# A decoder block in FP32 on one core: projections written as four column tiles, cross-attention score products of two heads per load of the queries, and a new order of the work

## The reference, cut to what matters

```
x = x + SelfAttention(layernorm(x))              # 16 heads of 16, rotary positions
x = x + CrossAttention(layernorm(x), ctx)        # 16 heads of 16, 77 context tokens
x = x + FFN(layernorm(x))                        # 6 nodes, each an attention of 8 heads of 32:
    q,k,v = linear functions of earlier nodes' outputs
    node  = act_w * (softmax(q k^T / sqrt(32)) v) @ Wo + q ;  at the end a layernorm with gain and shift
```

## Time and profile before

| | |
|---|---|
| median of 3 runs | 5278.08 us (5269.1 to 5292.41) |
| the profiled execution: its time | 5268.01 us |
| its span, first to last instruction | 5266.2 us |
| PE busy / PEld busy | 4823.1 us (92%) / 3530.9 us (67%) |
| DVE / ACT / POOL busy | 3453.1 us (66%) / 2479.3 us (47%) / 707.9 us (13%) |
| mean granted TensorE clock | 0.962 of full speed |
| PE matmul records / all instructions | 59612 / 149908 |

### The profile page before, as it was taken

One profiled execution on the slowest core, in us unless ns is written; L12 is line 12 of the kernel. 1 busy time (PEld: TensorE's weight loads), 2 busy tenths in 40 slices (PEclk: granted clock), 3 DMA queues, 4 the chain that ended last, 5 costly groups with the idle time before them and its releaser, 6 DMA issues.

```text
span 5266.2 us, 149908 instructions
## 1 busy us (share of the span) xinstructions
PE 4823.1 (92%) x59612; PEld 3530.9 (67%) x59612; DVE 3453.1 (66%) x6058; ACT 2479.3 (47%) x4737; POOL 707.9 (13%) x1734
## 2 busy tenths in 40 slices
PE   7998999989899898998989989899998989989898
PEld 6676766757667676666767667676675767757676
DVE  3666676666766667676676766667666676666765
ACT  1454444545455454454544445454454544545444
POOL 0102011020211102111020110202102021120201
PEclk8999999999999999998999999999999999999999
DMA  3000000000000000000000000000000000000000
GB/s 120 5 2 11 2 11 3 2 11 2 11 3 2 11 2 11 2 6 7 2 11 2 6 7 2 11 2 11 2 2 11 2 11 3 2 11 2 8 2 6
DMA packets 42888, 44.64 MB, mean 8 GB/s; under 512 B 11552, under 2 KB 41888, under 8 KB 42144
## 3 DMA queue, kind: packets, MB, share of 16 engines
q1 hardware_dynamic: 34192, 26.55, 1.7%
q10 hardware_dynamic: 7952, 7.81, 0.4%
HBM read 25.96 MB, written 8.39 MB: 7 GB/s over the span
## 4 chain that ended last, share of the span: by engine, by line
issue 55%; PE 28%; DVE 7%; POOL 6%; ACT 1%; POOLq 1%; DVEq 0%; ACTq 0%
PE banks L945 27%; DVE row_max L909 3%; POOL neg_max L719 2%; POOL neg_max L722 2%; POOL x_tok L704 1%; POOL inv_std L698 1%; PE banks L1064 1%; DVE pair_sums L930 1%; ACT probs L818 1%; DVE rope_s L874 1%; DVE k_parts L887 0%; POOL var_eps L695 0%; PE banks L994 0%; DVE n_tok L930 0%; DVE x_tok L942 0%
## 5 line engine op out<-in xcount | busy, mean ns | idle before, releaser
L909 DVE TENSOR_REDUCE row_max<-banks 128x4 f32<-128x1024 f32 (+1 forms) x1280 | 1313.3, 1068 | 350.5 <-PE banks L945 348.0
L818 ACT ACTIVATE probs<-banks 128x1024 f32<-128x1024 f32 (+1 forms) x1280 | 1137.8, 935 | 487.6 <-PE banks L945 469.9
L945 PE MATMUL banks<-k_parts,q_parts 32*128 32x256 f32 (+1 forms) x15360 | 652.1, 306 | 166.8 <-DVE row_max L909 130.9
L945 PEld LDWEIGHTS banks<-k_parts,q_parts 32*128 32x128 f32 x15360 | 541.9, 201 | 333.7 <-DVE row_max L909 162.4
L930 DVE TENSOR_TENSOR pair_sums<-probs 128x512 f32<-128x512 f32 x512 | 368.1, 719 | 524.3 <-ACT probs L818 403.3
L945 PE MATMUL banks<-q_parts,k_parts 32*128 32x256 f32 (+1 forms) x13824 | 605.4, 304 | 75.1 <-DVE row_max L909 32.0
L945 PEld LDWEIGHTS banks<-q_parts,k_parts 32*128 32x128 f32 (+1 forms) x13824 | 470.6, 188 | 291.6 <-issue 163.4
L719 POOL TENSOR_TENSOR neg_max<-row_max,zeros 128x8 fp32r<-128x8 f32 x640 | 166.4, 260 | 3680.1 <-DVE row_max L909 3680.1
L945 PE MATMUL banks<-node_t,w_n 128*128 128x256 f32 x2560 | 633.2, 390 | 5.5 <-ACT node_t L835 5.5
L930 DVE TENSOR_TENSOR n_tok<-probs 128x512 f32<-128x512 f32 x512 | 364.2, 711 | 286.7 <-PE banks L945 167.9
L945 PEld LDWEIGHTS banks<-node_t,w_n 128*128 128x128 f32 x2560 | 461.4, 190 | 125.2 <-issue 46.1
(11 more groups left out here) (130 smaller groups left out, 6491.7 us busy)
## 6 DMA issues: line engine op xcount, KB each, us to landing
x_next<-in_x SPq DMA_DIRECT2D x32, 256.0 KB, 2.7
out_y<-x_tok SPq DMA_DIRECT2D x32, 256.0 KB, 2.1
w_head<-in_wf SPq DMA_DIRECT2D x11, 256.0 KB, 10.9
c_t<-in_ctx_t SPq DMA_DIRECT2D x32, 77.0 KB, 2.9
w_edge_t<-in_we_t ACTq DMA_DIRECT2D x9, 256.0 KB, 10.9
w_head<-in_wf ACTq DMA_DIRECT2D x7, 256.0 KB, 9.3
w_edge_t<-in_we_t SPq DMA_DIRECT2D x6, 256.0 KB, 9.1
w_n<-in_we ACTq DMA_DIRECT2D x3, 256.0 KB, 11.5
```

What stands on the lines that cost most here:

```text
L818: done(act.activation(probs[s][0:rows, g % 2, 2 * p:2 * p + 2, 0:kt, :] .rearrange("p c k t -> p c (k t)"), psum[0:rows, b0:b0 + 2, 0:kt * T],
L909: done(dve.reduce_max(row_max[s][:, g, 2 * p:2 * p + 2, :].rearrange("p c q -> p (c q)"), psum[:, b0:b0 + 2, :].rearrange("p c (q t) -> p ...
L945: return nc.tensor.matmul(bank_ap, lhs, rhs, start=start, stop=stop, **kw)
```

## The change

There are four edits and a new list.

1. `matmul_by_columns` takes the place of one whole-array product by four with 32 columns of the stationary operand each, written to four quarters of the partitions. `Q`, `QB`, `K`, `V`, `QR`, `KR`, `OA` and `OB` use it. `TR` and `MT` keep the whole array. (For the values of the context, with 77 rows, there are three tiles.)
2. In stage 1, `S` and `SB` stream the keys of both halves of a strip (2 x 78 columns) for one load of the queries. The groups 1 and 3 of `S`, `SB`, `MX` and `NM` are gone there; `ST` and `SX` keep four groups.
3. `MX` in stage 1 reduces both heads in one instruction (2 banks x 4 maxima of 77), with the same two instructions per group.
4. `NM` in stage 1 splits the maxima of both heads at once.
5. `ORDER` is new: 922 pieces in place of 942, other banks, other neighbours.

```diff
+def score_groups(j):
+
+    return range(0, groups(j), 2 if j == CROSS else 1)
...
-KI0.1 LNP0.1 V1.0@5 LNN0.1 KS1.0 TR0.1@3 KH0.1 KL0.1 TRE0.1 KH1.0 KL1.0 Q0.1@6 QB0.1 QH0.1.0 QH0.1.1 QL0.1.1
-QL0.1.0 VE1.0 S1.0.0@0 SB1.0.0 MX1.0.0.0 MX1.0.0.1 S1.0.1@4 SB1.0.1 MX1.0.1.0 MX1.0.1.1 S1.0.2@0 SB1.0.2
-MX1.0.2.1 S1.0.3@4 SB1.0.3 MX1.0.3.0 MX1.0.2.0 NM1.0.2 MX1.0.3.1 S0.1.0@0 SB0.1.0 MX0.1.0.1 MX0.1.0.0 NM1.0.3
-S0.1.1@4 SB0.1.1 MX0.1.1.0 NM1.0.1 MX0.1.1.1 S0.1.2@0 SB0.1.2 MX0.1.2.0 NM1.0.0 MX0.1.2.1 S0.1.3@4 SB0.1.3
-MX0.1.3.1 MX0.1.3.0 MT1.0.0@0 MT1.0.1@2 MR1.0.0 MR1.0.1 NM0.1.1 NM0.1.3 ST1.0.0@4 SX1.0.0 ST1.0.1@0 SX1.0.1
...
+KI0.1 LNP0.1 LNN0.1 KS1.0 V1.0@3 TR0.1@4 KH0.1 KL0.1 TRE0.1 KH1.0 KL1.0 Q0.1@7 QB0.1 VE1.0 QH0.1.0 QH0.1.1
+S1.0.0@0 SB1.0.0 QL0.1.0 QL0.1.1 S1.0.1@4 SB1.0.1 MX1.0.0.0 MX1.0.1.1 MX1.0.0.1 MX1.0.1.0 XB0.1 NM1.0.1 S1.0.2@0
+SB1.0.2 MX1.0.2.0 MX1.0.2.1 NM1.0.2 NM1.0.0 S1.0.3@4 SB1.0.3 MX1.0.3.1 S0.1.0@0 SB0.1.0 MX0.1.0.1 MX0.1.0.0
+MX1.0.3.0 NM1.0.3 S0.1.2@0 SB0.1.2 MX0.1.2.0 MX0.1.2.1 MT1.0.0@5 MR1.0.0 ST1.0.0@4 MT1.0.1@1 SX1.0.0 MR1.0.1
+ST1.0.1@0 SX1.0.1 EX1.0.0.0 PA1.0.0.0 EX1.0.0.1 PA1.0.0.1 PV1.0.0@7 PS1.0.0 NM0.1.0 MT0.1.0@6 EX1.0.1.0
...
 
+        def pair_max(s, g):
+
+            return row_max[s][:, g:g + 2, :, :].rearrange("p a c q -> p (a c q)").rearrange("p (c m) -> p c m", c=4)
...
-                negated = row_max[s][:, g, :, :]
                 parts = neg_max[s][:, u, :, :].rearrange("p q (c r) -> p c q r", c=4)
+                high, low = parts[:, :, :, 2 * i], parts[:, :, :, 2 * i + 1]
+                negated, zero = row_max[s][:, g, :, :], zeros[:, :, 0:QT]
+                if j == CROSS:
+                    both = parts[:, :, :, 0:4].rearrange("p c q (e i) -> p c q e i", i=2)
+                    high, low = both[..., 0], both[..., 1]
+                    negated = pair_max(s, g).rearrange("p c (q e) -> p c q e", q=QT)
+                    zero = zeros[:, :, :].rearrange("p c (q e) -> p c q e", q=QT)
                 pool.wait_ge(sem["max_taken"], reached(at, "max_taken", ("MX", s, j, g, 0), ("MX", s, j, g, 1)))
-                done(pool.tensor_tensor(parts[:, :, :, 2 * i], negated, zeros[:, :, :], ALU.add),
-                     "max_split", (a, "high"))
+                done(pool.tensor_tensor(high, negated, zero, ALU.add), "max_split", (a, "high"))
                 pool.wait_ge(sem["max_split"], reached(at, "max_split", (a, "high")))
-                done(pool.tensor_tensor(parts[:, :, :, 2 * i + 1], negated, parts[:, :, :, 2 * i].bitcast(F32),
-                                        ALU.subtract), "max_split", (a, "low"))
+                done(pool.tensor_tensor(low, negated, high.bitcast(F32), ALU.subtract), "max_split", (a, "low"))
             elif k == "FG":
...
-                done(dve.reduce_max(row_max[s][:, g, 2 * p:2 * p + 2, :].rearrange("p c q -> p (c q)"),
-                                    psum[:, b0:b0 + 2, :].rearrange("p c (q t) -> p (c q) t", q=QT)
-                                    [:, :, 0:TC if j == CROSS else T], AX_X, negate=True), "max_taken", a)
+                if j == CROSS:
+                    maxima = pair_max(s, g)[:, 2 * p:2 * p + 2, :]
+                    scores = psum[:, b0:b0 + 2, 0:4 * TAIL].rearrange("p c (m t) -> p c m t", t=TAIL)[:, :, :, 0:TC]
+                else:
+                    maxima = row_max[s][:, g, 2 * p:2 * p + 2, :].rearrange("p c q -> p (c q)")
+                    scores = psum[:, b0:b0 + 2, :].rearrange("p c (q t) -> p (c q) t", q=QT)
+                done(dve.reduce_max(maxima, scores, AX_X, negate=True), "max_taken", a)
...
+        def matmul_by_columns(out_ap, lhs, rhs, start, stop):
+
+            rows = lhs.shape[-1]
+            for r in range(0, rows, ROWS):
+                last = nc.tensor.matmul(out_ap[r:min(r + ROWS, rows), :], lhs[:, r:min(r + ROWS, rows)], rhs,
+                                        start=start, stop=stop, skip_group_check=True)
+            return last
+
...
                 for d in range(KC):
-                    last = matmul(bank_of(a)[:, d * T:(d + 1) * T], w[:, c, d * P:(d + 1) * P],
-                                  node_input(s, j, "q")[:, c, :], c == 0 and d == 0, c == KC - 1,
-                                  skip_group_check=True)
+                    last = matmul_by_columns(bank_of(a)[:, d * T:(d + 1) * T], w[:, c, d * P:(d + 1) * P],
+                                             node_input(s, j, "q")[:, c, :], c == 0 and d == 0, c == KC - 1)
                 if k == "QB":
...
-                done(matmul(bank_of(a), rot[:, :], rope_in[s][:, :, :].rearrange("p k t -> p (k t)"), True, True),
-                     "proj_ready", a)
+                done(matmul_by_columns(bank_of(a), rot[:, :], rope_in[s][:, :, :].rearrange("p k t -> p (k t)"),
+                                       True, True), "proj_ready", a)
             elif k == "V":
                 if j == CROSS:
...
-                width = TAIL if j == CROSS else T
+                width = 2 * TAIL if j == CROSS else T
                 for q in range(QT):
                     for qp, kp in ((0, 0), (0, 1)) if k == "S" else ((1, 0),):
                         for c in range(4):
                             r = slice(ROWS * c, ROWS * (c + 1))
-                            last = matmul(psum[:, BANK[a][c], q * T:q * T + width],
-                                          q_parts[s][r, qp, x, q * P:(q + 1) * P],
-                                          parts[r, first + kp, x, 0:width], q == qp == kp == 0, k == "SB",
+                            keys = parts[r, kp:4:2, x, 0:TAIL] if j == CROSS else parts[r, first + kp, x, :]
+                            last = matmul(psum[:, BANK[a][c], q * width:(q + 1) * width],
+                                          q_parts[s][r, qp, x, q * P:(q + 1) * P], keys,
+                                          q == qp == kp == 0, k == "SB",
                                           tile_position=(ROWS * c, 0), skip_group_check=True)
                 if k == "SB":
                     done(last, "scores_ready", a)
             elif k == "MT":
...
-                                      for g in range(groups(j)) if place(j, g)[0] == u])
+                                      for g in score_groups(j) if place(j, g)[0] == u])
                 for q in range(QT):
...
-                        last = matmul(bank_of(a)[:, half * T:(half + 1) * T], lhs, rhs,
-                                      half == c == 0 and (k == "OA" or j < FFN0), k == "OB" and c == KC - 1,
-                                      skip_group_check=True)
+                        last = matmul_by_columns(bank_of(a)[:, half * T:(half + 1) * T], lhs, rhs,
+                                                 half == c == 0 and (k == "OA" or j < FFN0),
+                                                 k == "OB" and c == KC - 1)
                 if k == "OA" or a[3] == KC - 1:
                     done(last, "proj_ready", a)
```

147 lines of the change are left out of this document (73 added, 74 removed).

## The result

The changed kernel takes 5210.22 us (median of 4 runs, 5204.53 to 5220.34), the kernel before 5276.69 beside it. The ratio is 0.9876, with a 95% interval of 0.9856 to 0.9897: 66 us faster, not 141. That is just above the upper end of the range, 5210. The loop's first instruction starts at 142.3 us and its sixteenth turn at 4910.6, so a round takes 317.9 us on the mean; before it was (4965.6 - 138.7) / 15 = 321.8. So 3.9 us a round came, where 8.8 were forecast.

What follows compares the result with a forecast made beforehand. A round was taken as mostly a queue of TensorE steps, except about 40 us paced by VectorE's reductions. Terms 2.8 + 2.9 + 2.1 + 1.0 = 8.8 us, times 16 = 141, gave 5127 us from 5268; 8 in 10 for 5010 to 5210.

Steps and rivals of the forecast that it cites:

- changes of shape: Projections in column tiles: cheaper entries and exits between TensorE shapes save 2.8 us a round, bounds 1.8 and 3.9.
- two heads per load: Cross-attention scores: half the steps and wider reductions save 2.9 us a round in slot 0 and 2.1 in slot 1.
- the list: New order of pieces: its effect on the other waits taken as 0, with 4 us a round either way.
- the clock's -1.0: Half-speed time of 20.4 us a round: fewer, fuller narrow steps save 1.0 us a round, bounds 0 and 5.
- the arithmetic costs the same: Projections: four tiles of 32 columns take 0.21 us, one product of 128 columns 0.215; all 608 steps keep their price.
- the rival of the slower step: Long column-tile runs in the projections: steps of 0.24 us instead of 0.215 make the kernel slower, 5370 us; chance 0.05.
- The reduction's 0.79 us: VectorE, cross scores: two reductions of 308 elements become one of 616 at 0.79 us, bounded by 0.47 and 1.22.
- half of the groups go: Cross scores in slot 1: records taking 4.22 us lose half their groups, saving 2.1 us a round; 1.4 to 3.
- the price of a step in a long column run: Projections: 32 records behind another column shape take 0.215 us per four from the first step, and 1.75 after rows.
- the counts: Whole kernel: 87132 matmul records; 5930 DVE instructions, 128 fewer, with 128 reductions of 616 elements.
- the first rival: The clock's second fall does not come (3 us) and waits for `row_max` are halved: 16.8 us a round, 5000; chance 0.2.
- the entries saved turn into waits: Savings at shape changes become waits, so only the cross scores count, 5.0 us a round: 5188 us; chance 0.15.

Runs made afterwards that it cites:

- b_coltail_far: Kernel before, old list, column tiles in all projections but the six ahead of the jump, 28 needless small multiplications once ahead of the loop: 5237.71 us, ratio 0.9933.
- b_cross: Kernel before with only the cross-attention scores of two heads per load of the queries, whole-array projections, old list: 5251.73 us, ratio 0.9951.
- b_both_place: Kernel before with column tiles and two-head scores in the old list, plus 42 needless small multiplications once ahead of the loop: 5226.60 us, ratio 0.9910.
- a_place: Changed kernel with 42 needless one-column, one-row multiplications (168 instructions) once ahead of the loop, nothing else: 5164.24 us, ratio 0.9788 to the kernel before.
- b_both: Kernel before with column tiles in the projections and two-head scores, both in the old list: 5252.44 us, ratio 0.9949.
- a_whole: Changed kernel with its projections on the whole array again, new list kept: 5259.65 us, ratio 0.9977 to the kernel before.
- a_tail: Changed kernel with the six last projections of a round, ahead of the jump, kept on the whole array: 5150.47 us, ratio 0.9772 to the kernel before.
- a_edge: Changed kernel with V1.0, Q0.1, QB0.1 behind the jump and the six projections ahead of it on the whole array: 5147.68 us, ratio 0.9761 to the kernel before.
- b_near: Kernel before with 46 needless small multiplications (184 instructions) once ahead of the loop: 5340.65 us, ratio 1.0130.
- b_cols_place: Kernel before with column tiles in all projections, old list, plus 42 needless small multiplications once ahead of the loop: 5281.59 us, ratio 1.0014.
- b_coltail: Kernel before, old list, with column tiles in every projection but the six ahead of the jump: 5257.88 us, ratio 0.9969.

## Why the prediction was wrong

Per round (a difference of ratios times 5276 us, by 16), with intervals from those of the ratios:

| term | forecast | measured | from |
|---|---|---|---|
| changes of shape | -2.8 | -2.2 (-2.7 to -1.7) | b_coltail_far |
| two heads per load | -2.9 - 2.1 = -5.0 | -1.6 (-2.1 to -1.1) | b_cross |
| the list | 0 (4 either way) | -4.0 (-4.9 to -3.2) | b_both_place to a_place |
| stop inside `V1.0` | not in the sum | +2.9 (2.0 to 3.8) | a_place to the changed kernel |
| rest; a longer jump? | not in the sum | +0.8 (-0.1 to +1.8) | what is left in b_both_place |
| sum | -8.8 with the clock's -1.0 | -4.1 | |

The last term is what is left over and was not tested by itself; in the traces the last matrix multiplication ahead of the jump starts 2.41 us ahead of `V1.0` before, 3.74 in `b_both_place` and 3.34 in the changed kernel. Nor do the terms simply add up. The list brings 2.4 us (1.6 to 3.3) where both kernels have the stop (`b_both` to the changed kernel), 4.0 where neither has it, and without column tiles it costs 0.9 (`b_cross` to `a_whole`). The stop costs 1.3 us (0.5 to 2.0) in the old list (`b_both_place` to `b_both`) and 2.9 in the new one. Column tiles bring 2.2 in the old list and 6.8 (6.0 to 7.5) in the new one (`a_whole` to `a_tail`, which keeps six projections whole; neither has a stop). The table is one way through them.

**The step that failed** is "the arithmetic costs the same", with only the kind of the changes of shape to be priced. It priced 608 steps and forgot that they had become four times as many instructions, in another place of the program. I did look at the instruction queue, under the rival of the slower step, and only at its mean rate (0.7% of 16 engines' time). (The rate set beside it there is misstated: the 8 row records take 0.24 us, and 0.12 is the price of four. "Nearly twice the rate" is right.) A mean rate says nothing of one fetch that nothing covers: the loop's jump, once a round. The row for it was there before, 1.96 us of "issue" ahead of 1750.06, and I took it for a constant. The runs showed a stop inside the first projection behind the jump in its place, 2.9 us a round in the changed kernel. The change moved the end of the block from 194 to 51 instructions behind the loop's start, and these 51 are done before the next block is there.

**The mis-sized term** is the two heads. 1.6 us came of 5.0. The reduction's 0.79 us was right, and 2.4 of 2.9 us came in slot 0 of `b_cross` in the round shown, 1.7 on the mean. In the changed kernel that stretch is 12.8 us (1740.92 to 1753.75, forecast 11.9). In slot 1 the price was read off TensorE's own 4.22 us, "half of the groups go", and what was late next was not asked: VectorE's reductions, then the layer norm behind them on the same engine. 0.4 of 2.1 came in the round shown and nothing on the mean. Besides, `V1.0` to `TR0.1` takes 0.7 us more on the mean in `b_cross`, where the clock is at half behind the jump in 13 of 14 rounds, and in 5 before. In the changed kernel slot 0's gain is gone by the start: from `V1.0` to the first `ST` it is 22.5 us on the mean in both kernels.

**Right** were the price of a step in a long column run (0.216; the rival of the slower step is refuted), 1.73 and 1.75 us for 32 records, the counts, and the term for the changes of shape, within its bounds once neither stop hides it. The Trainium skill (TensorEngine Tiling (Array Packing), When to Use Tiling) advises column tiles for stationary operands of at most 64 columns. Here operands of 128 columns gained by them, 2.2 us a round in the old list, which the unchanged price of a step leaves to the changes of shape.

**The clock's term** came to nothing: the half-speed time is 20.7 us a round before and 20.5 after (mean clock 0.962 and 0.963). It moved, though. The second fall, 50 to 67 us behind `V1.0`, stood in all 14 rounds before and stands in 4 after, as the first rival had it. In its place came a fall at the jump, in 13 rounds and not 5. In `a_place`, without the stop, the half-speed time is 16.3 us and the mean clock 0.969.

**The list** was given 4 us either way, and it brought 4.0 between the two kernels without a stop; that this nearly cancels the two terms that were not in the sum is luck. Most of its gain is there by the start of `S1.2.0`, 84 us into a round (2.8 us between `b_both_place` and `a_place`); which wait it removes I did not settle. The waits for `row_max` rather grew (206.5 to 214.7 us in all). But the half-speed time falls from 23.6 to 16.3 us a round between the two, most of it at the second fall (7.3 to 1.0 us), and that is worth up to 3.7 us; whether that is the cause or comes of shorter waits is not shown. The rival "the entries saved turn into waits" gave 5188 and is nearest in time, but it was not the mechanism.

`a_tail` and `a_edge`, at 5150 and 5148 us, beat both kernels, and so does `a_place` with no change in the loop at all. Against `a_place`, the jump's idle time in `a_tail` falls from 2.92 to 1.40 us on the mean (0.70 in the round shown), but only 0.5 us a round comes of it (0.9788 to 0.9772, inside both intervals). Where the rest goes is not settled: from `V1.0` to `S1.2.0` both take the same (81.7 and 81.6 us).

## What to carry to other kernels

A change that multiplies the instructions of an engine in a loop has to be checked at the loop's jump: how long is "issue" there, how many instructions run behind it before the first gap, and is anything queued ahead of it that covers the fetch. A stop that cuts a uniform run of records at the same count round after round points to such an end of a block, and a few cheap instructions ahead of the loop test it in one run. What one edit brings depends on the list that it stands in, so it has to be measured there. And a saving on one engine is worth only what the next-late chain leaves: read it to the end of the stretch, not to the end of the engine's own work.

## What the hardware showed that I had not expected

- TensorE's program comes in blocks of 256 instructions (stops at the 1984th in `b_both` and the 1728th in `b_near`, none in `a_place`), and behind the loop's jump it goes on in the second block some 3 us after the first instruction runs (2.9 to 3.6 us behind the start of `V1.0` in `b_near`, 2.8 to 3.4 in the changed kernel). The Trainium skill says so much (Runtime: NRT & Kernel Launch, section "Instruction fetch mechanics"): blocks of 256 instructions, and a taken branch breaks the sequential prefetch. The traces agree. It also says that the fetch is otherwise hidden by the pace at which instructions are issued. These runs fit both: in the round shown of the changed kernel the 5.9 us of "issue" are all at the two jumps in it and at the stop (2.65, 2.80 and 0.47), and the stop costs 46 us of 5210.
- The jump itself took the same in the kernel before and after: the trace has the branch instruction 3.85 and 3.86 us ahead of the first `V1.0`, on the mean of 14 rounds. An instruction packet begins 1.0 to 1.1 us behind the branch, takes 1.1, and `V1.0` starts 1.6 to 1.7 us after it has landed. It is not the same everywhere: 4.8 us in `b_cols_place`, 5.05 in `b_coltail`, and 4.3 in `a_tail`, where 4 of 14 rounds take over 5.0.
- What differs between before and after is the work queued behind the branch: the last matrix multiplication starts 2.41 us ahead of `V1.0` in the kernel before, 3.34 after, 1.99 in `a_tail`. Short instructions give less cover than long ones. Between the branch and `V1.0` the trace has 20 instructions of TensorE before (weight loads and waits included), 19 to 21 after and 26 to 32 in `a_tail`; that the queue holds a fixed number of them is not shown.
- Behind a stop or a long jump, the granted clock often is at the lower of the two levels: 3.64 us for the 32 records of `V1.0` in `b_cols_place` against 1.93 in `a_place`. The stops of `b_near`, 2.1 us on the mean, cost 4.3 us a round (0.0130 x 5276 / 16).
